# One loop's step in another order: projection, numerators, scores, numerators, exponents

## What is computed

```python
x = x + cross_attention(layernorm(x), ctx)        # softmax attention, biases
x = x + causal_linear_attention(layernorm(x))     # 16 heads of 64, 128 features
x = x + ffn(layernorm(x))                         # ternary weights, 8-bit activations

# the middle stage, per head:
q, k, v = x @ Wq, x @ Wk, x @ Wv
phi(t) = exp(t @ W_feat - |t|^2 / 2) / sqrt(128)
num_t  = phi(q_t) @ sum_{s<=t} phi(k_s) v_s^T
den_t  = phi(q_t) . sum_{s<=t} phi(k_s) + 1e-6
y_t    = num_t / den_t ;   out = y @ Wo
```

## Time and profile before

| | us |
|---|---|
| median of 3 runs | 253.41 (253.39 to 253.46) |
| the profiled execution | 253.28 |
| its span, first to last instruction | 251.5 |
| PE busy | 239.7 (95%) |
| DVE busy | 187.6 (75%) |
| ACT busy | 146.5 (58%) |
| POOL busy | 101.6 (40%) |
| loop, project(1) to project(15) | 81.38 to 177.28 |

### The profile page before, as it was taken

How to read it: one execution, slowest core, us unless ns; L and a number is a source line. 1 busy time by engine, 2 the same in 40 slices (tenths; PEclk the granted TensorE clock), 3 DMA queues, 4 the chain that set the end, 5 groups by cost and what they waited for, 6 DMA issues and landing times.

```text
span 251.5 us, 6988 instructions
## 1 busy us (share of the span) xinstructions
PE 239.7 (95%) x2722; PEld 188.8 (75%) x2728; DVE 187.6 (75%) x476; ACT 146.5 (58%) x284; POOL 101.6 (40%) x139
## 2 busy tenths in 40 slices
PE   7998889999999999999999999999999989999984
PEld 7854556777788778787777878777789978888863
DVE  5577888666742685777888888775688979999994
ACT  0554454534446888567656766765647257787772
POOL 2063113342202558344674578726720024444430
PEclk9999999999999999999999999999999999999999
DMA  7999999990079001100110000000000000000001
GB/s 189 357 390 404 398 395 393 344 390 33 1 252 330 4 0 46 44 3 1 44 44 3 1 3 3 3 0 3 4 3 3 4 0 3 21 23 21 22 26 63
DMA packets 15377, 26.83 MB, mean 107 GB/s; under 512 B 1232, under 2 KB 8688, under 8 KB 15344
## 3 DMA queue, kind: packets, MB, share of 16 engines
q1 hardware_dynamic: 14576, 25.96, 28.9%
q10 hardware_dynamic: 768, 0.43, 0.6%
HBM read 25.33 MB, written 1.05 MB: 105 GB/s over the span
## 4 chain that ended last, share of the span: by engine, by line
PE 63%; DVE 18%; issue 6%; POOL 5%; ACT 4%; DMA 2%; SPq 0%; DVEq 0%; POOLq 0%; ACTq 0%
PE b L1346 11%; PE b L1106 7%; PE b L1390 6%; PE b L1108 6%; PE b L1107 6%; PE b L1365 4%; PE b L1267 3%; PE b L1270 2%; PE b L1263 2%; DMA xwk<-in_xWk 2%; PE b L1520 2%; DVE yT_lo L980 2%; DVE xn L742 2%; PE b L1218 2%; PE b L1186 2%
## 5 line engine op out<-in xcount | busy, mean ns | idle before, releaser
L852 DVE TENSOR_TENSOR x_lo<-b,x_hi 128x512 fp32r<-128x512 f32 x32 | 21.7, 688 | 16.8 <-ACT x_hi L463 16.7
L600 ACT ACTIVATE phi<-b 128x512 f32<-128x512 f32 x48 | 26.0, 597 | 11.3 <-PE b L1346 11.3
L403 POOL TENSOR_TENSOR sq_lo<-sq_sum,sq_hi 128x512 fp32r<-128x512 f32 x16 | 20.6, 1287 | 25.8 <-ACT sq_hi L463 25.8
L345 POOL TENSOR_TENSOR lnr<-lnv,mh 128x1 f32<-128x1 f32 x16 | 8.8, 552 | 54.9 <-DVE lnv L716 54.7
L521 ACT ACTIVATE sq<-b 128x512 f32<-128x512 f32 x32 | 19.3, 603 | 18.1 <-PE b L1108 18.1
L397 POOL TENSOR_TENSOR sq_sum<-sq,sq 128x512 f32<-128x512 f32 x16 | 20.7, 1293 | 21.6 <-ACT sq L521 21.6
L1106 PE MATMUL b<-nT_lo,wp_hi 128*128 128x512 f32 x64 | 26.8, 418 | 0.1
L1108 PE MATMUL b<-nT_hi,wp_hi 128*128 128x512 f32 x64 | 25.0, 391 | 0.0
L1107 PE MATMUL b<-nT_hi,wp_lo 128*128 128x512 f32 x64 | 25.0, 390 | 0.0
L926 DVE TENSOR_TENSOR smk<-b,mask 64x512 f32<-64x512 f32 x32 | 22.0, 688 | 2.9 <-PE b L1365 1.2
L1390 PEld LDWEIGHTS b<-va,smk 128*64 128x64 f32 x512 | 17.5, 137 | 7.5 <-issue 7.1
(11 more groups left out here) (180 smaller groups left out, 615.9 us busy)
## 6 DMA issues: line engine op xcount, KB each, us to landing
cT<-in_ctxT SPq DMA_DIRECT2D x8, 1028.0 KB, 14.0
cn<-in_ctx SPq DMA_DIRECT2D x8, 1024.0 KB, 14.7
wv_raw<-in_aWv SPq DMA_DIRECT2D x1, 1024.0 KB, 13.8
wp_raw<-in_aWq SPq DMA_DIRECT2D x4, 256.0 KB, 4.0
wp_raw<-in_aWk SPq DMA_DIRECT2D x4, 256.0 KB, 4.2
w_raw<-in_w2T SPq DMA_DIRECT2D x1, 1024.0 KB, 5.4
wo<-in_aWo SPq DMA_DIRECT2D x1, 1024.0 KB, 7.9
w_raw<-in_w1T SPq DMA_DIRECT2D x1, 1024.0 KB, 5.0
```

What stands on the lines that cost most here:

```text
L403: nc.gpsimd.tensor_tensor(sq_lo[n % 2][:], sq_sum[:], sq_hi[n % 2][:].bitcast(F32), ALU.subtract).then_inc(sq_l, 1)
L600: nc.scalar.activation(phi(n, a)[:], feature_bank(a), ACT.Exp).then_inc(f_exp, 1)
L852: nc.vector.tensor_tensor(x_lo[n % 2][r][:], proj_bank(n, r), x_hi[n % 2][r][:].bitcast(F32), ALU.subtract).then_inc(x_l, 1)
```

## The change

PE's step becomes: project(n); slot(n) (numerators, scores, numerators); exponents(n-1). ACT's step becomes: squares(n, 0), the exponentials of heads 2 and 3 of step n-2, squares(n, 1), squares_high(n), the exponentials of heads 0 and 1 of step n-1. head_order is gone, heads go 0, 1, 2, 3 everywhere, and attention(u) waits for just the exponentials that it reads. DVE's step: low(n, 0), outputs(2u-2), low(n, 1), masked(u), outputs(2u-1). weight_scales and its w_bc matmuls stand at the head of step 4. Behind the loop: numerators 24 to 27 together, exponents(15), both transposes of group 0, attention(14); attention(15) and numerators 28 and 29 in the middle of project_out(0), numerators 30 and 31 behind it. ACT takes yTc(0, .) between the two pairs of exponentials of step 15 and loads the table for Gelu after them. Score 14 goes to b3. Numbers of instructions are unchanged.

```diff
@@ -591,7 +588,7 @@
             def features(n, *at):
                 j = n // 2
                 for k in at:
-                    a = head_order(n)[k]
+                    a = k
                     if a < 2 and j >= 1:
                         act.wait_ge(s_mm, 2 * (j - 1) + 1)
                     if a >= 2 and j >= 2:
@@ -602,12 +599,12 @@
             squares_high(0)
             for n in range(1, STEPS):
                 squares(n, 0)
+                if n >= 2:
+                    features(n - 2, 2, 3)
                 squares(n, 1)
+                squares_high(n)
                 features(n - 1, 0, 1)
-                squares_high(n)
-                features(n - 1, 2, 3)
-            features(STEPS - 1, 0, 1, 2, 3)
-
+            features(STEPS - 2, 2, 3)
 
             def yTc(g, c):
                 if g >= 2:
@@ -661,9 +658,11 @@
                 act.wait_ge(x2_cp, LAST)
                 copy(res[:, LAST, :], b2[:, 0:D]).then_inc(x2_cp, 1)
 
-            nc.scalar.activation(spare[:], mh[:, 0:2], ACT.Gelu)
+            features(STEPS - 1, 0, 1)
             yTc(0, 0)
             yTc(0, 1)
+            features(STEPS - 1, 2, 3)
+            nc.scalar.activation(spare[:], mh[:, 0:2], ACT.Gelu)
             act.wait_ge(s_mask, 2 * STEPS)
             for i in range(NG + 1):
                 if i + 1 < NG:
@@ -951,9 +950,12 @@
                     ALU.mult).then_inc(n_y, 1)
 
             for n in range(1, STEPS):
-                low(n, 0)
                 if n == 4:
                     weight_scales()
+                low(n, 0)
+                u = n - 3
+                if u >= 1:
+                    outputs(2 * u - 2)
                 low(n, 1)
                 if n == 1:
                     dve.wait_ge(ld_mask, 16)
@@ -961,9 +963,6 @@
                     weight_sum(1, w2_raw[:], ld_w2)
                 if n == 2:
                     weight_sum(0, w1_raw[:], ld_w1)
-                u = n - 3
-                if u >= 1:
-                    outputs(2 * u - 2)
                 if u >= 0:
                     masked(u)
                 if n == STEPS - 1:
@@ -983,9 +982,9 @@
 
             for v in range(24, 28):
                 outputs(v)
-            masked(14)
             yTc(0, 0)
             yTc(0, 1)
+            masked(14)
             masked(15)
             for v in range(28, 32):
                 outputs(v)
@@ -1333,15 +1332,15 @@
 
 
             def exponents(n):
-                h, order = n % 2, head_order(n)
+                h = n % 2
                 pe.wait_ge(x_l, 2 * n + 2)
                 pe.wait_ge(sq_l, n + 1)
                 terms = [(w[:, r], v[h][r]) for w, v in ((feat_hi, x_hi), (feat_lo, x_hi), (feat_hi, x_lo))
                          for r in range(2)] + [(neg_half[:], sq_hi[h]), (neg_half[:], sq_lo[h])]
                 for k, (w, v) in enumerate(terms):
-                    for a in order:
+                    for a in range(QUAD):
                         if k == 0 and n >= 1:
-                            pe.wait_ge(f_exp, 4 * (n - 1) + head_order(n - 1).index(a) + 1)
+                            pe.wait_ge(f_exp, 4 * (n - 1) + a + 1)
                         rows = slice(HR * a, HR * (a + 1))
                         mm = pe.matmul(feature_bank(a), w[rows], v[rows, :], start=(k == 0), stop=(k == len(terms) - 1))
                         if k == len(terms) - 1:
@@ -1349,10 +1348,7 @@
 
             def attention(u):
                 j, pair = u // 2, u % 2
-                if u < 14:
-                    pe.wait_ge(f_exp, 8 * (j + 1))
-                else:
-                    pe.wait_ge(f_exp, 2 * (u - 14) + 62)
+                pe.wait_ge(f_exp, 8 * j + 2 * pair + 6)
                 if u < 13:
                     pe.wait_ge(s_mask, 2 * u)
                 if u == 13:
@@ -1403,15 +1399,15 @@
                     numerators(2 * u - 1)
 
             for n in range(1, STEPS):
+                if n == 4:
+                    pe.wait_ge(w_sum, 2)
+                    pe.matmul(b7[:, 508:510], neg_half[:].bitcast(F32), wsum[:, 0:2], start=True, stop=True).then_inc(w_bc, 1)
                 project(n, 0, 1)
                 if n == 1:
                     pe.wait_ge(v_cp, 2 * NG)
-                if n == 4:
-                    pe.wait_ge(w_sum, 2)
-                    pe.matmul(b7[:, 508:510], neg_half[:].bitcast(F32), wsum[:, 0:2], start=True, stop=True).then_inc(w_bc, 1)
-                exponents(n - 1)
                 if n >= 3:
                     slot(n)
+                exponents(n - 1)
 
             def yTt(g, c):
                 pe.wait_ge(n_y, 2 * H - QUAD if g < HALF else 2 * H)
@@ -1422,17 +1418,12 @@
                                       ident[:])
                 mm.then_inc(yT_mm, 1)
 
-            numerators(24)
-            numerators(25)
+            for v in range(24, 28):
+                numerators(v)
             exponents(STEPS - 1)
-            numerators(26)
-            numerators(27)
-            attention(14)
             yTt(0, 0)
             yTt(0, 1)
-            attention(15)
-            numerators(28)
-            numerators(29)
+            attention(14)
 
 
             def project_out(g):
@@ -1444,13 +1435,17 @@
                     pe.matmul(b2[:, 0:D], ident[:], res[:, g, :], start=True, stop=False)
                 for c in range(HC):
                     if g == 0 and c == 4:
-                        numerators(30)
-                        numerators(31)
+                        attention(15)
+                        numerators(28)
+                        numerators(29)
                     if c % 4 == 0:
                         pe.wait_ge(yT_d, 2 * g + 1 + c // 4)
                     mm = three(b2[:, 0:D], yT_hi[g % 2][:, c, :], yT_lo[g % 2][:, c, :], wo_hi[:, c, :],
                                wo_lo[:, c, :], c == 0 and g < LAST, c == HC - 1)
                 mm.then_inc(o_mm, 1)
+                if g == 0:
+                    numerators(30)
+                    numerators(31)
 
             def aqTt(g):
                 if g == 0:
@@ -1521,7 +1516,6 @@
                                    stop=(c == HC - 1))
                 mm.then_inc(f2_mm, 1)
 
-            pe.wait_ge(f_exp, 4 * STEPS)
             for i in range(NG + 1):
                 if i + 1 < NG:
                     yTt(i + 1, 0)
```

More of the change, by code:

```diff
@@ L196, in score_bank @@
         def score_bank(u):
-            return {13: b0[:], 14: b2[:], 15: b4}.get(u, b6)
+            return {13: b0[:], 14: b3[:], 15: b4}.get(u, b6)
         def value_bank(v):
             return {23: b1[:], 25: b6, 26: b1[:], 27: b0[:], 29: b3[:], 30: b5, 31: b6}.get(v, b7)[:, 0:HALF * VW]
-        def head_order(n):
-            return (2, 3, 0, 1) if n < STEPS - 1 else (0, 1, 2, 3)
         def phi(n, a):
```

## The result

| | before | after |
|---|---|---|
| median of 12 runs | 253.4 us | 255.81 us (255.33 to 256.48) |
| ratio, with its 95% interval | 1 | 1.0088 [1.0073, 1.0104] |
| the profiled execution, its span | 253.28, 251.5 | 256.48, 254.7 |
| project(2) | 84.90 | 85.20 |
| project(5) | 103.93 | 104.71 |

The change makes the kernel slower by 2.4 us; 255.0 had been forecast, 1.6 more. The profiled execution of after is the longest of its 12 runs; behind the last matmul row it has 0.7 us more than before, so that row gives the comparison best: 2.49 us later. These are 0.30 ahead of project(2), in code that is the same, 0.48 from there to project(5), 0.02 in the ten steps of the loop, 1.69 behind the loop, and nothing after project_out(1): from there to the last matmul row it is 48.13 us in both.

What follows compares the result with a forecast made beforehand. The prediction took PE to bound the loop and a chain through DVE the stretch behind it. Start +0.3, loop -0.2 and end +1.5 summed to +1.6 us, giving 255.0 us; own range 254.3 to 255.8, full range 253.4 to 256.4.

Steps and rivals of the forecast that it cites:

- What bounds the kernel: Whole kernel: the loop belongs to PE, busy 72.38 of 73.35 us; DVE is busy 17.73 of the next 22.32.
- The loop: Ten steps from project(5) to project(15): a step of 7.33 us against 7.35, together -0.2 us, bounds -1.4 to +0.7.
- Rival 2: In the loop: changes of array shape are cheap and the stall shrinks, step 6.92 us, time 251.1; chance 0.11.
- The start: First steps up to project(5): exponents(1) waits for exponentials now behind squares(2,0); +0.3 us, range 0 to +0.6.
- The end: Behind project(15): late scores(15) and numerators put the second group's yT_lo at T+22.64, before T+21.12; +1.5 us, bounds 0.8 and 2.2.
- The table load: ACT's load for Gelu, moved behind the last exponentials: costs nothing, and leaving its old place brings nothing.
- Rival 1: Behind the loop: gaps after project_out(1) absorb the end's delay, time 253.8 us or less; chance 0.12.
- Rival 3: In the eight loop steps with quantise_w: POOL holds DVE up and PE with it, +1.0 us, time 256.0; chance 0.11.

Runs made afterwards that it cites:

- e4: Kernel before, with PE's exponents moved between the first numerators and the scores; 252.47 us, ratio 0.996.
- e5: Changed kernel, with PE's exponents moved between the scores and the second numerators; 255.18 us, ratio 1.0073.
- e8: e6, with ACT's exponentials and DVE's outputs of the last loop steps also at their old places; 254.08 us, ratio 1.0016.
- e1: Changed kernel, but ACT takes all four exponentials of step 0 in a row in step 1; 255.36 us, ratio 1.0071.
- e2: Changed kernel with its loop, but the order behind the loop rewritten as in the kernel before; 254.74 us, ratio 1.0044.
- e6: Changed kernel's order in loop steps 2 to 14, old start, exponents(14) ahead of slot(15), old order behind the loop; 254.45 us, ratio 1.0044.
- e3: Kernel before with its loop, but the changed kernel's whole order behind the loop; 255.85 us, ratio 1.0085.
- e9: e3, but with scores(14) ahead of the transposes of group 0 as in the kernel before; 256.12 us, ratio 1.0083.

## Why the prediction was right

The time lies inside the range and at the upper edge of the forecast's own one (255.8). The mechanism was right at both ends and, for the loop, in that it hardly changes. Each term came out 0.2 us or so above its forecast; the errors have one sign, so none made good for another.

- **What bounds the kernel.** Right. PE sets the loop, and the chain through DVE sets its end.
- **The loop, -0.2 forecast, 0.02 longer measured.** Of the pieces, project to numerators was forecast at 0.33 and took 0.32, scores to numerators 1.20 and 1.19, exponents to project 0.35 and 0.33. The mis-sized piece is numerators to exponents: 0.56 forecast, 0.62 measured (109.41 to 110.03), its upper bound. In a usual step (step 10, from 141.42) the others are 0.06 shorter together and make good for it: it takes 7.33, as summed. The -0.2 itself came from holding that sum against step 5's 7.35, where the mean of the ten steps before was 7.335; against the mean it would have been -0.05. Rival 2 did not come; the stall stays, as e4 and e5 confirm from the other side: it shrank when exponents was put in it. e8 confirms the neutral loop by its time.
- **The start, +0.3 forecast, +0.48 measured.** The cause is shown by e1. Step 2 was forecast at 5.80 and took 5.85, step 3 at 6.23 and took 6.32 (85.20, 91.05, 97.37), step 4 at 7.33 and took 7.34: the layout was right, and its small errors all had one sign.
- **The end, +1.5 forecast, +1.69 measured.** The layout held point by point, from T: numerators(23) 5.62 (forecast 5.48), exponents(14) 6.23 (6.04), exponents(15) 10.31 (10.3), scores(14) 13.67 (13.6), scores(15) 16.95 (16.87), masked(15) 18.15 (18.07), yT_lo 22.80 (22.64), project_out(1) 24.01 (23.8). What the forecast left open is which part causes it. By the distance from T to yT_lo (22.80 in after, 21.12 before) the order behind the loop holds 0.86 (e2, 21.94). exponents(14) at its old place brings nothing by itself (e6, 22.16); with ACT's and DVE's old order of step 15 the distance is 21.44 (e8). So about 0.5 of the loss hangs on these together, and the last 0.3 goes with the new order of the heads, by e8's trace alone. The medians of e2, e6 and e8 differ from each other hardly by more than their intervals; only the first part and the total are firm.
- **The table load costs nothing.** Right: it stands at 193.68, 1.28 us long, and ACT's next instruction waited 2.49 us for masked(15) even so. No run moved it alone.
- **Rival 1, the delay absorbed.** Wrong, as weighed: from project_out(1) to the last matmul row it is 48.13 us in both kernels; the chain has no slack at all.
- **Rival 3, DVE late in the quantise steps.** Its condition came, its price did not. The prediction had L845 as not held up, from one row of 0.75; in the same trace two of the eight took 1.11. In after, the same operation (L844) took 1.66 us in steps 9 and 10, and DVE went on to low without a gap:

```profile
142.36 1.35 POOL L410 TENSOR_TENSOR wo_lo<-wo,wo_hi 128x512 fp32r<-128x512 f32 x1
142.60 1.66 DVE L844 SCALAR_TENSOR_TENSOR w2q<-w_raw,wsum,w2q 128x512 bf16<-128x512 f32 x1
144.23 0.69 DVE L851 TENSOR_TENSOR x_lo<-b,x_hi 128x512 fp32r<-128x512 f32 x1
```

The Trainium skill, "SBUF — State Buffer", Who interferes with whom, has the shared port pair as exclusive; the trace agrees, as L844, elsewhere 0.75 to 0.77 us long, lasts until 0.55 us after the end of POOL's operation. But low(10,0) starts 2.81 us behind project(10) (141.42), as in the other steps: the slack of 0.3 us was used up and just sufficed. Of the eight steps with quantise_w, step 5 took 7.37 and the others 7.33 to 7.34.
- **The rest.** 0.3 us stand ahead of project(2), in code that the change leaves as it was, and e1's trace (project(2) at 84.86) has nothing of it. It is taken as scatter between executions, not as a part of the change. Without it the terms give 2.2 us; the medians are 2.4 apart, and the 0.2 between them isn't assigned.

The e-runs show a reading weaker than the forecast: the expectations of e3, e5, e6 and e9 followed only one chain. Each time a wait of 0.5 to 1.6 us stood on another one, where an engine waited for work that had been moved or that kept its old place.

## What to carry to other kernels

Another order of a steady loop was worth nothing here, as the bounding engine's distances from start to start add up to the same; what it does to the first and the last steps, where the loop's cover is missing, decided. A wait that has moved with its chain is not removed: it goes when an independent block as long as the wait stands between the two instructions that share the buffer (7.33 to 7.17 a step here). When one engine's order is changed near the end, lay out all three queues again before pricing it, since the cover of one wait can be the work just moved, as in e9.

## What the runs showed of the hardware

One more change of the array's shape in a step costs little: numerators to exponents is 0.09 to 0.10 us over numerators' own pitch of 0.52, and in e4 a step with four changes is shorter than one with three. The Trainium skill, "TensorEngine Tiling (Array Packing)", Key Properties, says that a change of mode drains TensorE. The rows agree so far as each of the changes measured costs something: this one 0.10, exponents to project 0.33 against a pitch of 0.23.

A wait inside a group of short matmuls shows in no bracket. It is seen only in the row's length and in the distance to the next row (1.56 and 1.18 in after, 1.59 and 1.20 in e6, against 0.74 and 0.57).
